# Residual add walked by channel, groups written out, and the seam product in four column tiles

## What is computed

```python
    # --- layer 0 (conv_preact) ---
    x = x + _L0_conv_ref(_gn(x), L0_conv_u, L0_conv_v, L0_conv_w, L0_conv_b)
    # --- layer 1 (conv_preact) ---
    x = x + _L1_conv_ref(_gn(x), L1_conv_u, L1_conv_v, L1_conv_w, L1_conv_b)
```

## Time and profile before

| | |
|---|---|
| median of three runs | 5806.66 us |
| profiled execution, first to last instruction | 5804.7 us |
| PE busy | 5183.7 us (89%) |
| DVE busy | 4447.4 us (77%) |
| ACT busy | 3444.0 us (59%) |
| DMA | mean 96 GB/s |
| granted TensorE clock, mean | 0.994 of full speed |

### The profile page before, as it was taken

How to read it: one execution, slowest core, us unless ns; L and a number is a source line. 1 busy time by engine, 2 the same in 40 slices (tenths; PEclk the granted TensorE clock), 3 DMA queues, 4 the chain that set the end, 5 groups by cost and what they waited for, 6 DMA issues and landing times.

```text
span 5804.7 us, 93109 instructions
## 1 busy us (share of the span) xinstructions
PE 5183.7 (89%) x30720; PEld 3991.0 (69%) x30720; DVE 4447.4 (77%) x7315; ACT 3444.0 (59%) x5377; POOL 25.9 (0%) x25
## 2 busy tenths in 40 slices
PE   6899989899898988988989889898989889899997
PEld 5766766677666776776667676676667766776675
DVE  6777777777777777777777777777777777777776
ACT  4556655566566655655556556665566556655664
POOL 1000000000000000000000000000000000000000
PEclk9999999999999999999999999999999999999999
DMA  2212222112222212221122212222122222122211
GB/s 121 119 61 90 90 119 119 79 74 88 119 119 90 87 64 119 119 101 79 67 114 119 117 63 81 99 119 119 67 85 90 119 119 90 67 85 119 119 61 61
DMA packets 53095, 556.71 MB, mean 96 GB/s; under 512 B 7008, under 2 KB 19808, under 8 KB 19808
## 3 DMA queue, kind: packets, MB, share of 16 engines
q10 hardware_dynamic: 33728, 520.10, 21.7%
q1 hardware_dynamic: 18848, 29.93, 1.6%
HBM read 268.99 MB, written 268.44 MB: 93 GB/s over the span
## 4 chain that ended last, share of the span: by engine, by line
PE 53%; DVE 40%; issue 6%; ACT 0%; DMA 0%; DVEq 0%; SPq 0%; ACTq 0%
DVE image L428 31%; PE ps_b L314 30%; PE ps_z L283 15%; DVE z L417 9%; PE ps_t L269 6%; PE ps_b L311 1%; PE ps_s L323 0%; ACT transposed L349 0%; DMA image<-in_x 0%; DVE bn L440 0%; ACT relu L392 0%; DVEq L416 0%; DVE band L210 0%; DVE relu L207 0%; DVE small L475 0%
## 5 line engine op out<-in xcount | busy, mean ns | idle before, releaser
L283 PE MATMUL ps_z<-mix,transposed 128*128 128x160 f32 (+2 forms) x17408 | 2596.0, 292 | 490.3 <-DVE z L417 478.5
L283 PEld LDWEIGHTS ps_z<-mix,transposed 128*128 128x128 f32 x17408 | 2327.6, 191 | 651.7 <-DVE z L417 567.1
L349 ACT ACTIVATE transposed<-ps_t,norm 128x512 f32<-128x512 f32 (+1 forms) x2304 | 1724.3, 755 | 1129.7 <-PE ps_t L269 1127.5
L428 DVE TENSOR_TENSOR image<-image,relu 128x512 f32<-128x512 f32 x2048 | 2066.5, 1061 | 16.1 <-DMA relu<-seam_r 16.1
L314 PE MATMUL ps_b<-z,band 128*128 128x512 f32 x4096 | 1840.5, 598 | 14.7 <-ACT z L364 2.5
L392 ACT ACTIVATE relu<-ps_b,parameters 128x512 f32<-128x512 f32 x2048 | 1409.4, 688 | 478.7 <-PE ps_b L314 466.1
L417 DVE COPY z<-ps_z 128x480 f32<-128x480 f32 (+1 forms) x1536 | 1017.6, 663 | 832.9 <-PE ps_z L283 832.8
L269 PE MATMUL ps_t<-shift,image 128*128 128x128 f32 x8704 | 1334.6, 274 | 74.3 <-issue 37.1
L314 PEld LDWEIGHTS ps_b<-z,band 128*128 128x128 f32 x4096 | 757.9, 190 | 847.5 <-issue 830.3
L440 DVE BATCH_NORM_STATS2 bn<-image 128x6 f32<-128x512 f32 x2048 | 1256.3, 695 | 17.4 <-DMA image<-in_x 17.4
L269 PEld LDWEIGHTS ps_t<-shift,image 128*128 128x128 f32 x8704 | 1036.3, 142 | 149.7 <-issue 74.5
(11 more groups left out here) (38 smaller groups left out, 248.1 us busy)
## 6 DMA issues: line engine op xcount, KB each, us to landing
out<-image ACTq DMA_DIRECT2D x64, 4096.0 KB, 11.6
image<-in_x ACTq DMA_DIRECT2D x60, 4096.0 KB, 13.4
image<-in_x SPq DMA_DIRECT2D x4, 4096.0 KB, 27.7
seam_z<-z SPq DMA_DIRECT2D x256, 32.0 KB
relu<-seam_r SPq DMA_DIRECT2D x256, 16.0 KB, 2.1
shift<-in_shifts SPq DMA_DIRECT2D x1, 192.0 KB, 2.4
z<-in_seams SPq DMA_DIRECT2D x1, 192.0 KB, 2.6
parameters<-in_params SPq DMA_DIRECT2D x2, 66.0 KB, 2.1
```

The source lines that it names most:

```text
L283: last = nc.tensor.matmul(ps_z[i % PS_Z][:, (a - lo) * C:(z + 1 - lo) * C], T[:, i % T_SLOTS, n * P:(n + 1) * P], mix[layer_of(k)][:, a - ...
L349: nc.scalar.activation(T[:, i % T_SLOTS, 0:n], ps_t[i % PS_T][:, 0:n], ACT.Identity, scale=norm[:, k % 2, 0:1], bias=norm[:, k % 2, 1:2]). ...
L428: nc.vector.tensor_tensor(x_px, x_px, R[:, :, s, w0:w0 + ADD_PX].rearrange("p c w -> p w c"), ALU.add).then_inc(added, 1)
```

## The change

Three edits. The add walks channels outside and pixels inside: R is now read in runs of 32 neighbours, and X is read and written with a step of 16 elements (64 bytes). All 16 groups are written out, and every wait has a constant. The seam's product becomes four, each with 64 rows and 32 columns of the weights on 64 pixels, into the four quarters of the PSUM partitions; its ReLU works on 128 partitions of 64 pixels; and the way back to R is eight DMAs of 4 KB instead of two of 16 KB, all waited for by the first add.

```diff
+SEAM_PARTS = 4
+SEAM_W = W // SEAM_PARTS
...
-        seam_r = sb("seam_r", [2 * C, W])
+        seam_r = sb("seam_r", [SEAM_PARTS * 2 * C, SEAM_W])
...
-            group(0, True, False)
-            with eng.Fori(1, GROUPS - 1) as t:
-                group(t, False, False)
-            group(GROUPS - 1, False, True)
+            for t in range(GROUPS):
+                group(t, t == 0, t == GROUPS - 1)
...
                     for r, (p, s) in enumerate(((P - 1, 0), (0, 1))):
-                        sp.dma_start(R[p:p + 1, :, s, :], seam_r[r * C:(r + 1) * C, :]).then_inc(seam_out, 16)
+                        for q in range(SEAM_PARTS):
+                            sp.dma_start(R[p:p + 1, :, s, q * SEAM_W:(q + 1) * SEAM_W],
+                                         seam_r[(2 * q + r) * C:(2 * q + r + 1) * C, :]).then_inc(seam_out, 16)
...
-                            nc.tensor.matmul(ps_b[m % PS_B][:, 0:W], seam_w[y][:], seam_z[:],
-                                             start=True, stop=True).then_inc(banded, 1)
+                            for q in range(SEAM_PARTS):
+                                part_done = nc.tensor.matmul(ps_b[m % PS_B][2 * C * q:2 * C * (q + 1), 0:SEAM_W],
+                                                        seam_w[y][0:4 * C, 0:2 * C],
+                                                        seam_z[0:4 * C, q * SEAM_W:(q + 1) * SEAM_W],
+                                                        start=True, stop=True)
+                            part_done.then_inc(banded, 1)
...
-                            nc.scalar.activation(seam_r[:], ps_b[m % PS_B][0:2 * C, 0:W], ACT.Relu,
-                                                 bias=par[y][0:2 * C, PARAMS - 1:PARAMS]).then_inc(relued, 1)
+                            nc.scalar.activation(seam_r[:], ps_b[m % PS_B][0:SEAM_PARTS * 2 * C, 0:SEAM_W], ACT.Relu,
+                                                 bias=par[y][0:SEAM_PARTS * 2 * C, PARAMS - 1:PARAMS]).then_inc(relued, 1)
...
                 if c == 0:
-                    dve.wait_ge(seam_out, value(2 * 16, t, k, 2 * 16))
-                x_px = X[buf_of(k % JOBS)][:, s, w0 * C:(w0 + ADD_PX) * C].rearrange("p (w c) -> p w c", c=C)
-                nc.vector.tensor_tensor(x_px, x_px, R[:, :, s, w0:w0 + ADD_PX].rearrange("p c w -> p w c"),
-                                        ALU.add).then_inc(added, 1)
+                    dve.wait_ge(seam_out, value(2 * SEAM_PARTS * 16, t, k, 2 * SEAM_PARTS * 16))
+                x_ch = X[buf_of(k % JOBS)][:, s, w0 * C:(w0 + ADD_PX) * C].rearrange("p (w c) -> p c w", c=C)
+                nc.vector.tensor_tensor(x_ch, x_ch, R[:, :, s, w0:w0 + ADD_PX], ALU.add).then_inc(added, 1)
```

## The result

The changed kernel takes 6097.39 us (median of four runs, 6090.19 to 6097.86) against 5805.65 us before (median of four runs): 1.0503 of the time, 95% interval 1.0489 to 1.0518. The profiled execution spans 6095.2 us. That is 292 us slower; 173 us slower were forecast. The direction, the mechanism and the whole range (5650 to 6360 us) held; the size did not, and the forecast's own range (5850 to 6080 us) is missed by 17 us.

The account below looks back on a forecast made before the run. PE and DVE were taken to alternate, with DVE setting the pace from the first add on. 5804.7 - 56 + 216 + 0 + 12 = 5977, given as 5979 us; own range 5850 to 6080, whole range 5650 to 6360.

Parts of the forecast that it names:

- one for one, down to PE's own pace: Pixel phase: from the first add on, whatever DVE gains or loses moves the job's end equally, until PE limits.
- Part 1: Group loop: writing out all groups removes the 13 loop turns, -56 us (bounds -56 to -50); constant waits bring nothing.
- Part 2: Seam's way back to R: eight DMAs land 1.55 us after the first add is due, +216 us (+80 to +250).
- the term for late landings: Seam DMAs landing late while an image is on its way: one job in four at 1 us, taken as +15 us.
- Part 3: Add on DVE: cost goes with single elements and only moves from R to X; unchanged at 0.97 us, 0 us.
- the low bound: Add: single elements cost 0.53 ns instead of 0.72, so 0.87 us an add, -200 us, 5779 us; chance 0.15.
- Part 4: Seam's products on PE and ReLU: eight small records take 0.52 us, +12 us in all (-38 to +58).
- the usual delay: First add of a usual job: waits 1.55 us for the last seam landing, 127 times, +197 us.
- the last job's 4 us: After the last job: nothing hides the seam DMAs, +4 us.
- The free read of X: Rival, add: reading X at 64 bytes costs nothing, 0.60 us an add, about 5300 us; chance 0.11.
- the disturbed write: Rival, add: read and write of X disturb each other, 6730 us, or 6350 at half; chance 0.15.
- The hidden DMAs: Rival, seam: eight DMAs issued below 0.39 us each stay hidden, add unchanged, 5763 us; chance 0.07.

## Why the prediction was right, and where it missed

**What bounds the kernel.** Right for a delay of the first add. DVE's added waiting before it turned up in the time nearly in full: 290.7 us as 299 with eight DMAs, 153.8 as 152 with the load later. For work taken off DVE behind the first add, "one for one, down to PE's own pace" did not hold (216 us expected, 158 gained).

**Part 1, the loop.** Right: 56 us forecast, 53 measured, and no gain from constants.

**Part 2, the way back.** The mechanism was right: eight issues, the last landing behind the time the add is due, DVE idle before each first add. For a usual job, 1.55 us were forecast; 1.39 came (0.63 us an issue instead of 0.60, but a landing of 1.78 instead of 2.1 us), 127 x 1.39 = 177 us against 197. (By its own terms the forecast landing is 2507.28 + 4.2 + 2.1 = 2513.58, 1.49 us late, 189 us.) The step that failed is the term for late landings, put at +15 us: it measured 192 us, and with it part 2 came to 369 us, outside its bounds of +80 to +250. It is two terms. The slow issues are worth 40 us; the row that shows them, up to 1656 ns for L243, was read only for its median. The load in front of the last seam DMA is worth 152 us. The prediction took 3.8 us, the longest landing before, as what a landing takes "when an image is on its way". The trace of before says otherwise: the landing takes over 2.5 us in 25 jobs, in each of them a 16 KB transfer of the instruction queue runs beside it, and in none a transfer of an image. That row had no price for a load in it. In that kernel both DMAs are out 0.6 us after the last ReLU, and the load comes 4.7 us or more after it. Spreading the issues over 4.4 us or more moved the last across the load, and its landing went to 7.3 us. Whether it falls before or behind is a matter of 0.3 us (4.39 against 4.69), which is why a slow issue of 1 us costs 5 us in a job with a load (first add 11.5 us after the first issue on the mean of the 34, instead of 6.2). The question that the forecast left out is what else is issued in the longer stretch.

**Part 3, the add.** The number was right (unchanged duration; 24 us gained by a closer spacing), and the way to it was right only in part. That the cost goes with the single element and not with the distance is confirmed. That scattered writes are free was read from L417, which has one input; in the add they cost as much as reads. It did no harm only because the costs do not add. And L457, the row behind the low bound, has one input too; why it takes 17 ns more than L459 is open: the one-input forms above lie within 11 ns of each other (608 to 619), but none has its operands in order.

**Part 4, the product.** Forecast +12 us within -38 to +58, measured about +1. The four tiles do run side by side (0.25 us for eight records), and what going to small tiles and back costs, which no row could price, takes it back.

**Sum.** From the written-out kernel: 5752 - 24 (add) + 177 (usual delay) + 40 (slow issues) + 152 (behind a load) + 1 (tiles) = 6098, measured 6097. Of the forecast's miss of 118 us, the load and the slow issues are 177 too low; the usual delay (20 too high), the add (24), the tiles (11) and the last job's 4 us take back 59. The last job's did come (its add waits 19.6 us instead of 16.2), and is no term of its own in this sum.

**The rivals.** The free read of X did not happen (1062 ns). Nor did the low bound (0.87 us an add; 0.956 came), nor the disturbed write: 1062 ns with X read and written at 64 bytes, 1038 and 1045 with one of the two. The hidden DMAs exist with four of them, not with eight. So the case that was called the forecast is the one that happened, 17 us above its range; that 6097 us lies within 5650 to 6360 is luck in part, since the upper end was set by half of a disturbed write and not by anything in part 2.

## What to carry to other kernels

When one transfer becomes several, the last landing is what the waiting engine sees: count the issues, take their spacing from the queue, and then look at what other large transfers are issued in the stretch that has become longer. A maximum in the profile of before is no bound for a transfer that moves to another time, and it is no price either until one has looked at what ran beside it: here it was a transfer of instructions, and not the image it was taken for. Slack of 2 us, invisible in a list of waits, decided here between nothing and 5%.

## What had not been expected of the hardware

- A two-input float32 operation of 512 elements on DVE takes 692 ns with all operands in order and 1038 to 1105 ns with any operand at single elements, 16 bytes to 2 KB apart, read or written. One-input operations take 608 to 619 ns whether the write alone or read and write are scattered; none was run in order. The Trainium skill (SBUF — State Buffer, Door 1: The DMA port swizzle) lets each access to a new line of 16 bytes pay; the two-input forms agree (0.7 ns an element), and for the one-input forms no run shows it either way.
- Going to 64x32 tiles and back costs 0.31 us beside 128x128 products; four such tiles of 64 pixels take 0.25 us together, against 0.55 us for one of 256.
- SP's issues of small DMAs take 0.59 us at the median and up to 1.72 us in some jobs. In the changed kernel the slow ones come in six jobs of sixteen, in the written-out kernel with two DMAs in 10 of 128. Each of them overlaps a 16 KB transfer of instructions and ends 0.30 to 0.40 us after it. Why such a transfer falls into the issues in some jobs and not in others is open.
